# Context attention: the maximum over eight part maxima and the exponent's offset in one vector instruction, issued one copy later

## The chip, the core and the metric

The kernel runs on one core of one Trainium2 chip. The core has five engines that work side by side and meet through semaphores: PE (TensorE, matrix products), DVE (VectorE), ACT (ScalarE), POOL (GpSimd) and SP (SyncE, which here issues the DMAs). The metric is the device time of one execution in microseconds (us).

## What is computed

The reference is one perceiver layer: cross attention of 4 x 128 rows on a context of 8192 rows with 16 heads of 64, then a causal self attention, then a feed-forward layer with 4-bit weights. The change lies in the cross attention. Cut to that:

```
def _L0_xattn_ref(x, cond, Wq, bq, Wkv, bkv, Wp, bp):
    q = (x @ Wq + bq).reshape(1, B * N, H, hd)
    kv = (cond @ Wkv + bkv).reshape(1, -1, 2, H, hd)
    q = _fq_sym(q * scale, axis=-1)      # round to 127 levels per row and head
    k = _fq_sym(k, axis=-1)
    v = _fq_sym(v, axis=2)
    attn = softmax(einsum('bhqd,bhkd->bhqk', q, k), axis=-1)
    attn = _fq_unsigned(attn, axis=-1)   # scale so that the row's largest is 255, round
    out = einsum('bhqk,bhkd->bhqd', attn, v)
    return out @ Wp + bp
```

The kernel keeps q as integers and gives each score row a factor s (the row's query scale over K_SCALE). A probability in units of the row's largest/255 is exp(s * score + bias) with bias = ln 255 - s * (largest score of the row). LN_TOP is ln 255. The exponential is written as a 16-bit integer, which does the rounding.

## The kernel before

`attend_quantised` works in 64 **units** of one head (16) and 128 query rows (4 per head, T = 4). The score row of a unit has 8192 columns, cut in CH = 8 chunks of 1024. Two score rows (`at_sc0`, `at_sc1`) and two score banks in PSUM (`at_score0`, `at_score1`) are used in turn. For each unit:

- PE (`scores`) fills a bank with two 512-column products. It waits until the bank's last reader, two chunks earlier, is done.
- DVE (`copy`, L1508) copies the chunk from PSUM to `at_sc` and takes its maximum on the way into one column of `at_pmax`. In the trace this is a TENSOR_SCALAR_CACHE_REDUCE and a DVE_READ_ACCUMULATOR, which puts the maximum into SBUF. The chunks go in ORDER 2, 3, 6, 7, 4, 0, 1, 5; I call the copies p0 to p7 after their place in it. Each waits for its bank (`filled`) and for whoever still reads that part of `at_sc` for the unit two earlier: the exponentials, the DMA transpose, or PE's turns.
- DVE (`find_max`, L1513) reduces the eight part maxima to the negative maximum `at_nmax`, and (`make_bias`, L1520) turns it into `at_bias`. Both stand directly behind copy p7, and each waits for the instruction ahead of it.
- ACT (`exps`, L1598) takes the exponential of the two halves of the row in place, once `at_bias` is there. Behind each half stand two copies of the unit before, from PSUM to SBUF (`turned_out`, L1605).
- Half of each probability row is turned by a DMA transpose, the other half by PE in four groups (`turns`, k = 0 to 3, L1399), and PE multiplies them with the values (L1408, L1420). A turn k waits for `turned_out` of turn k - 2.
- Once per head, DVE also sums the row sums (`total_sum`, L1525), inverts them (L1529) and scales the output (L1535).

The order on each engine is written out by hand: `body(i, ...)` goes over the SLOTS = 8 units of one pair of heads and for each over c = 0 to 7. At slot c DVE copies chunk c + AHEAD (AHEAD = 2), so at c = 5 comes copy p7 of unit n + 1, and at c = 6 copy p0 of unit n + 2. The first and the last pair are written out, and the six pairs between them (48 units) run in a hardware loop, `Fori`, in which counts that grow with i are made in registers; DVE then has REGISTER_ALU and waiting instructions of its own between the copies.

POOL fetches each head's query columns and factors (`fetch`, `at_qs` from `exp_scale`, L1336), and quantises the values. `exp_scale` is made once, by `Queries.scales` (L639) in the key stage, more than 1100 us earlier.

Of the kernel before, what the change touches and what calls it, by code (L numbers as in the profile page):

```python
# [14 lines left out]
ALU = mybir.AluOpType  # L15
ACT = mybir.ActivationFunctionType
AX = mybir.AxisListType
F32 = mybir.dt.float32
# [4 lines left out]
P = 128  # L23
B, S, D = 4, 128, 1024
T = B * S // P
HEADS, HD = 16, 64
# [4 lines left out]
X_SCALE, W_SCALE, K_SCALE = 16.0, 256.0, 64.0  # L31
# [107 lines left out]
class Turner:  # L139
# [39 lines left out]
    def part(self, t, h):  # L179
        return slice(None), slice(4 * h, 4 * h + 4), slice(t * P, (t + 1) * P)  # L180
# [435 lines left out]
class Queries:  # L616
# [9 lines left out]
    def maximum(self, dve, t):  # L626

        self.nc.vector.tensor_reduce(self.amax[:, t, :], heads_of(self.q[:, t, :]), AX.X, ALU.max,
                                     apply_absolute_value=True).then_inc(self.scaled, 1)

    def scales(self, dve):

        nc = self.nc
        dve.wait_ge(self.scaled, T)
        nc.vector.tensor_scalar(self.scale[:], self.amax[:], HD ** -0.5 / LEVELS, 1e-8, ALU.mult, ALU.max)\
            .then_inc(self.scaled, 1)
        dve.wait_ge(self.scaled, T + 1)
        nc.vector.reciprocal(self.inv[:], self.scale[:]).then_inc(self.scaled, 1)
        nc.vector.tensor_scalar(self.exp_scale[:].rearrange("p h t -> p t h"), self.scale[:], 1.0 / K_SCALE, None,  # L639
                                ALU.mult).then_inc(self.scaled, 1)  # L640
        dve.wait_ge(self.scaled, T + 2)
        nc.vector.tensor_scalar(self.inv[:], self.inv[:], HD ** -0.5, None, ALU.mult).then_inc(self.scaled, 1)

    def divide(self, dve, t):

        dve.wait_ge(self.scaled, T + 4)
        rows = heads_of(self.q[:, t, :])
        self.nc.vector.tensor_tensor(rows, rows, per_head(self.inv[:, t, :]), ALU.mult).then_inc(self.scaled, 1)

    def round(self, dve):  # L650

        dve.wait_ge(self.scaled, 2 * T + 4)
        self.nc.vector.tensor_scalar(self.q[:], self.q[:], MAGIC, MAGIC, ALU.add, ALU.subtract).then_inc(self.scaled, 1)

    def scalar(self, act, c):

        act.wait_ge(self.scaled, 2 * T + 5)
        self.nc.scalar.activation(self.twice[:, :, :, c, :], self.q[:].rearrange("p t (h d) -> p t h d", d=HD),
                                  ACT.Copy).then_inc(self.step, 1)
# [549 lines left out]
def attend_quantised(chip, q_t, exp_scale, heads, v_scale, col, twice, o, ident32, ident16, x_d, x, stores, panels):  # L1209
# [7 lines left out]
    nc = chip.nc  # L1217
    SLOTS = 2 * T
    SC = 1024
    CH = NKV // SC  # L1220
# [3 lines left out]
    AHEAD = 2  # L1224
    LN_TOP = float(np.log(255.0))

# [7 lines left out]
    v_step, filled, copied = chip.sem("at_v_steps"), chip.sem("at_filled"), chip.sem("at_copied")  # L1234
    bias_ready, bias_step, exp_done = chip.sem("at_bias_ready"), chip.sem("at_bias_steps"), chip.sem("at_exp")
    dma_turned = [chip.sem(f"at_dma_turned{j}") for j in range(2)]
# [7 lines left out]
    COPIED0, EXP0, TURNED0, DMA0, OUT0, SUMMED0, DSUM0, INV0, TAKEN0, MOVED0 = 2, 4, 8, 16, 2, 4, 2, 4, 2, 2  # L1244
    with ExitStack() as ctx:
# [3 lines left out]
        q_pair = [chip.sb(ctx, f"at_q{j}", [P, T * P], F16) for j in range(2)]  # L1249
        qs_pair = [chip.sb(ctx, f"at_qs{j}", [P, T], F32) for j in range(2)]  # L1250
        vs_pair = [chip.sb(ctx, f"at_vs{j}", [P, HD], F32) for j in range(2)]
        vi_head = chip.sb(ctx, "at_vi", [P, HD], F32)
        o_pair = [chip.sb(ctx, f"at_o{j}", [P, T, HD], F32) for j in range(2)]
        part_max = [chip.sb(ctx, f"at_pmax{j}", [P, CH], F32) for j in range(2)]
        neg_max = [chip.sb(ctx, f"at_nmax{j}", [P, 1], F32) for j in range(2)]
        bias = [chip.sb(ctx, f"at_bias{j}", [P, 1], F32) for j in range(2)]
# [234 lines left out]
        def _(dve):  # L1491
# [18 lines left out]

            def find_max(h, n):
                dve.wait_ge(copied, COPIED0 + (h + 1) * CH)
                nc.vector.tensor_reduce(neg_max[n % 2][:], part_max[n % 2][:], AX.X, ALU.max, negate=True)\  # L1513
                    .then_inc(bias_step, 1)

            def make_bias(h, n):

                dve.wait_ge(bias_step, h + 1)
                j, t = (n % SLOTS) // T, n % T
                nc.vector.tensor_scalar(bias[n % 2][:], neg_max[n % 2][:], qs_pair[j][:, t:t + 1], LN_TOP,  # L1520
                                        ALU.mult, ALU.add).then_inc(bias_ready, 1)

# [15 lines left out]
            def body(i, first, last):  # L1538
                for n in range(SLOTS):
                    g = i * SLOTS + n  # L1540
                    for c in range(CH):
                        ahead, pos = (n + 1, c + AHEAD) if c + AHEAD < CH else (n + 2, c + AHEAD - CH)
# [3 lines left out]
                        j = (n // T + 1) % 2  # L1546
# [4 lines left out]
                        if done is not None and n % T == 1 and c == 4:  # L1551
                            output(done, j)
                        if c == 5 and not (last and ahead >= SLOTS):
                            find_max(i * SLOTS + ahead, ahead)
                            make_bias(i * SLOTS + ahead, ahead)

            for c in range(CH + AHEAD):
# [12 lines left out]
                if c == CH - 1:  # L1570
                    dve.wait_ge(q_ready, 2)
                    find_max(0, 0)
                    make_bias(0, 0)
# [669 lines left out]
def build(nc, a, out_d):  # L2243
# [11 lines left out]
    with chip.all, ExitStack() as whole:  # L2255
# [10 lines left out]
        with ExitStack() as cross:  # L2266
            q_t = chip.sb(cross, "q_t", [P, HEADS, T * P], F16)
            exp_scale = chip.sb(cross, "exp_scale", [P, HEADS, T], F32)
            v_scale = chip.sb(cross, "v_scale", [P, 2, D], F32)
# [150 lines left out]
```

## Time and profile before

| | us |
|---|---|
| median of 3 runs | 2665.52 (2664.87 to 2669.96) |
| span of the profiled execution | 2664.4 |
| PE busy in the span | 2483.9 (93%) |
| DVE busy in the span | 2035.2 (76%) |
| context attention, first to last `at_bias` | 1338.5 to 1967.6 |

The page gives the profiled execution by its span, from the first to the last instruction; the median lies 1.1 us above that. "Busy" counts the time of an engine's own instructions. Matrix products are pipelined and their ends modelled, so a busy PE need not be the limit. A bracket at the end of a timeline row is the idle time ahead of the instruction and whoever ended it.

### The profile page before, as it was taken

The numbers are of one execution on the slowest core, as the hardware profiler recorded it, in microseconds if no ns is written. First come the engines' busy times: TensorE is split into PE (matmuls) and PEld (weight loads), VectorE is DVE, ScalarE is ACT, GpSimd is POOL, SyncE is SP. The second block draws the span as 40 slices with busy tenths as digits, with TensorE's granted clock in tenths as the row PEclk, the third lists the DMA queues.
The fourth block names the chain that finished last, engine by engine and source line by source line (L and its number), as shares of the span: only waits on it lengthen the run. The fifth ranks groups of instructions, "written<-read, shape, count | busy, mean of one in ns | idle before, by whom it ended". The sixth has DMA issues, their size and how long they took to land. (4 is left out here: it accounts for less than half of the span.)

```text
span 2664.4 us, 42948 instructions
## 1 busy us (share of the span) xinstructions
PE 2483.9 (93%) x16296; PEld 1281.4 (48%) x16296; DVE 2035.2 (76%) x2932; ACT 1093.7 (41%) x1171; POOL 873.8 (33%) x432
## 2 busy tenths in 40 slices
PE   6999999999999999999978888888869999999998
PEld 3444444444444444444445555555544458444444
DVE  7898878778777877877699999999966344666664
ACT  4222222222222222222289999999982125211101
POOL 0233222322322232232166566566541651011100
PEclk9999999999999999999999999999999985999999
DMA  6234443443453344344479989989982331000000
GB/s 261 58 88 122 126 105 92 126 117 88 110 134 104 85 126 117 97 109 126 113 198 218 223 200 214 222 201 212 222 230 83 118 79 35 1 16 16 1 4 32
DMA packets 557347, 321.57 MB, mean 121 GB/s; under 512 B 401968, under 2 KB 533296, under 8 KB 552368
## 3 DMA queue, kind: packets, MB, share of 16 engines
q1 hardware_dynamic: 557232, 319.91, 47.0%
q8 instruction: 87, 1.43, 0.2%
q14 instruction: 28, 0.23, 0.0%
HBM read 149.95 MB, written 69.21 MB: 82 GB/s over the span
## 5 line engine op out<-in xcount | busy, mean ns | idle before, releaser
L1508 DVE TENSOR_SCALAR_CACHE_REDUCE at_sc<-at_score 128x1024 f32<-128x1024 f32 x512 | 597.1, 1220 | 12.5 <-PE at_score L1388 7.9
L1598 ACT ACTIVATE at_sc<-at_sc,at_bias,at_qs 128x4096 uint16<-128x4096 f32 x128 | 486.5, 3800 | 19.1 <-DVE at_bias L1520 18.4
L881 PE MATMUL kv_vacc<-wt_stage,kv_xthi 128*128 128x512 f16 x1024 | 388.1, 379 | 1.3 <-PEq L282 1.3
L881 PE MATMUL kv_vacc<-kv_wlo,kv_xthi 128*128 128x512 f16 x1024 | 388.1, 379 | 0.0
L881 PE MATMUL kv_vacc<-wt_stage,kv_xtlo 128*128 128x512 f16 x1024 | 388.1, 379 | 0.0
L889 PE MATMUL kv_kacc<-kv_wk,q_t 128*128 128x512 f16 x1536 | 347.2, 379 | 0.0
L960 ACT ACTIVATE q_t<-q_t 128x512 f16<-128x512 f32 x128 | 77.3, 628 | 488.9 <-POOL q_t L1163 327.8
L1161 POOL TENSOR_TENSOR q_t<-kv_rows 128x512 f32<-128x512 f32 x32 | 40.9, 1279 | 690.8 <-DMA kv_rows<-in_ctx 610.2
L889 PEld LDWEIGHTS kv_kacc<-kv_wk,q_t 128*128 128x128 f16 x1536 | 150.3, 98 | 181.2
L966 ACT ACTIVATE o<-wt_stage 128x1024 f16<-128x1024 f32 x64 | 67.7, 1058 | 407.0 <-DVE wt_stage L1052 407.0
L889 PE MATMUL kv_kacc<-kv_wk,kv_xthi 128*128 128x512 f16 x768 | 228.4, 379 | 0.7 <-DVE kv_xtlo L738 0.7
L1063 DVE SCALAR_TENSOR_TENSOR wt_stage<-kv_vacc,kv_bias 128x512 f32<-128x512 f32 x128 | 87.8, 686 | 175.9 <-PE kv_vacc L881 168.8
L1388 PE MATMUL at_score<-x,at_q 128*128 128x512 f16 x512 | 157.4, 390 | 61.2 <-DVE at_sc L1508 49.0
L1033 DVE SCALAR_TENSOR_TENSOR wt_stage<-kv_kacc,wt_stage 128x512 f32<-128x512 f32 x224 | 150.9, 686 | 80.6 <-PE kv_kacc L889 77.4
L1388 PE MATMUL at_score<-wt_stage,at_q 128*128 128x512 f16 x512 | 154.8, 384 | 53.6 <-DVE at_sc L1508 45.9
L1346 POOL TENSOR_TENSOR wt_stage<-wt_stage,at_vi 128x2048 f32<-128x2048 f32 x32 | 145.5, 4546 | 126.3 <-DMA wt_stage<-values 126.3
L1399 PEld LDWEIGHTS at_turn<-ident,at_sc 128*128 128x128 f16 x2048 | 136.4, 98 | 62.5 <-ACT at_sc L1598 2.9
L1028 DVE SCALAR_TENSOR_TENSOR q_t<-q_t 128x512 f16<-128x512 f32 x128 | 158.7, 1279 | 7.0 <-ACT q_t L960 7.0
L1174 POOL TENSOR_TENSOR wt_stage<-wt_stage,kv_bias 128x1024 f32<-128x1024 f32 x32 | 87.3, 2730 | 230.0 <-DVE wt_stage L1033 230.0
L1399 PE MATMUL at_turn<-ident,at_sc 128*128 128x128 f16 x2048 | 157.1, 220 | 3.2 <-ACT at_probt L1605 3.2
L881 PEld LDWEIGHTS kv_vacc<-wt_stage,kv_xthi 128*128 128x128 f16 x1024 | 100.2, 98 | 122.2 <-issue 1.7
L881 PEld LDWEIGHTS kv_vacc<-wt_stage,kv_xtlo 128*128 128x128 f16 x1024 | 100.2, 98 | 120.8
(246 smaller groups left out, 4242.6 us busy)
## 6 DMA issues: line engine op xcount, KB each, us to landing
kv_rows<-in_ctx SPq DMA_DIRECT2D x64, 512.0 KB, 7.0
values<-wt_stage SPq DMA_DIRECT2D x32, 1024.0 KB, 6.4
keys_turned<-o SPq DMA_DIRECT2D x32, 1024.0 KB, 5.1
wt_stage<-values SPq DMA_DIRECT2D x16, 2048.0 KB, 8.8
wt_stage<-keys_turned SPq DMA_DIRECT2D x32, 512.0 KB, 5.1
x<-keys_turned SPq DMA_DIRECT2D x31, 512.0 KB, 5.1
x<-in_x SPq DMA_DIRECT2D x2, 2048.0 KB, 8.6
kv_wk<-in_wq SPq DMA_DIRECT2D x2, 2048.0 KB, 12.7
```

Of the source, the lines that this page charges most:

```text
L881: last = nc.tensor.matmul(v_acc[2 * s + c][:], a[s][:, k, :], b[:, c, k, :], start=(k == 0 and q == 0), stop=(k == KD - 1 and q == 2))
L889: last = nc.tensor.matmul(k_acc[bank][:], a[:, k, :], b[:, k, :], start=(k == 0 and q == 0), stop=(k == KH - 1 and q == 2))
L960: nc.scalar.activation(s_hi[:, n], s_rows[:, n], ACT.Copy, scale=X_SCALE).then_inc(s_hi_ready, 1)
L1028: nc.vector.scalar_tensor_tensor(out=s_lo[:, n], in0=s_rows[:, n], scalar=X_SCALE, in1=s_hi[:, n], op0=ALU.mult, op1=ALU.subtract).then_in ...
L1033: nc.vector.scalar_tensor_tensor(out=out, in0=k_acc[bank][:], scalar=UNSCALE, in1=other, op0=ALU.mult, op1=ALU.add).then_inc(k_taken, 1)
L1063: nc.vector.scalar_tensor_tensor(out=val[:, h:h + HALF // HD, s, :], in0=v_acc[2 * s + c][:].rearrange("p (h d) -> p h d", d=HD), scalar=U ...
L1174: nc.gpsimd.tensor_tensor(key[:, 0, :], key[:, 0, :], bias[:, 0:D], ALU.add)\
L1346: nc.gpsimd.tensor_tensor(v_raw[:, tiles], v_raw[:, tiles], vi_head[:].unsqueeze(1).to_broadcast((P, KVT // 2, HD)), ALU.mult).then_inc(v_ ...
L1388: last = nc.tensor.matmul(score[pos % 2][:, b * HALF:(b + 1) * HALF], q_pair[j][:, t * P:(t + 1) * P], kt[j][:, cols], start=True, stop=True)
L1399: last = nc.tensor.transpose(turn[BANK[k]][:, b, :], prob[n % 2][1][:, at:at + P].bitcast(F16), ident16[:])
L1508: nc.vector.tensor_scalar(sc[n % 2][:, c * SC:(c + 1) * SC], score[pos % 2][:], 1.0, None, ALU.mult, ALU.max, accum_out=part_max[n % 2][:, ...
L1598: nc.scalar.activation(prob[n % 2][e], sc[n % 2][:, e * EC:(e + 1) * EC], ACT.Exp, bias=bias[n % 2][:], scale=qs_pair[j][:, t:t + 1], accu ...
```

## The change

The two small DVE instructions per unit become one `tensor_tensor_reduce`: it adds one column to the eight part maxima, multiplies by another, and takes the minimum. With c1 = -LN_TOP/s and c2 = -s, (m + c1) * c2 = LN_TOP - s * m, and its minimum over the parts is the bias. As a program it is two instructions, the main one and one that reads the accumulator into `at_bias`. It is issued at c = 6 instead of c = 5, behind copy p0 of the next unit but one; its wait for the copies stands with a semaphore increment of its own (`bias_begun`) ahead of it. `exp_scale` becomes three times as wide, with the two added columns from `Queries.scales`, and `at_qs` holds 12 elements instead of 4.

```
 class Queries:
+    def part(self, n):
+        return self.exp_scale[:, :, n * T:(n + 1) * T].rearrange("p h t -> p t h")
...
     def scales(self, dve):
...
-        nc.vector.tensor_scalar(self.exp_scale[:].rearrange("p h t -> p t h"), self.scale[:], 1.0 / K_SCALE, None,
-                                ALU.mult).then_inc(self.scaled, 1)
+        nc.vector.tensor_scalar(self.part(0), self.scale[:], 1.0 / K_SCALE, None, ALU.mult).then_inc(self.scaled, 1)
         dve.wait_ge(self.scaled, T + 2)
+        nc.vector.tensor_scalar(self.part(1), self.scale[:], -1.0 / K_SCALE, None, ALU.mult).then_inc(self.scaled, 1)
+        nc.vector.tensor_scalar(self.part(2), self.inv[:], -K_SCALE * LN_TOP, None, ALU.mult).then_inc(self.scaled, 1)
+        dve.wait_ge(self.scaled, T + 5)
...
-            def find_max(h, n):
-                dve.wait_ge(copied, COPIED0 + (h + 1) * CH)
-                nc.vector.tensor_reduce(neg_max[n % 2][:], part_max[n % 2][:], AX.X, ALU.max, negate=True)\
-                    .then_inc(bias_step, 1)
-
-            def make_bias(h, n):
-
-                dve.wait_ge(bias_step, h + 1)
+            def make_bias(h, n):
+
+                dve.wait_ge(copied, COPIED0 + (h + 1) * CH)
+                dve.sem_inc(bias_begun, 1)
                 j, t = (n % SLOTS) // T, n % T
-                nc.vector.tensor_scalar(bias[n % 2][:], neg_max[n % 2][:], qs_pair[j][:, t:t + 1], LN_TOP,
-                                        ALU.mult, ALU.add).then_inc(bias_ready, 1)
+                nc.vector.tensor_tensor_reduce(shifted[n % 2][:], part_max[n % 2][:],
+                                               qs_pair[j][:, 2 * T + t:2 * T + t + 1].to_broadcast((P, CH)),
+                                               qs_pair[j][:, T + t:T + t + 1], LARGEST, ALU.add, ALU.min,
+                                               bias[n % 2][:]).then_inc(bias_ready, 1)
...
-                        if c == 5 and not (last and ahead >= SLOTS):
-                            find_max(i * SLOTS + ahead, ahead)
-                            make_bias(i * SLOTS + ahead, ahead)
+                        if c == 6 and not (last and n + 1 >= SLOTS):
+                            make_bias(i * SLOTS + n + 1, n + 1)
```

How the instructions stand on DVE inside the loop, at the first unit of a head (the row sums of the head before are taken here). Before:

```order
L1508 TENSOR_SCALAR at_sc,at_pmax<-at_score 128x1024
L1524 ISA
L1525 TENSOR_REDUCE at_total<-at_psum 128x4
L1512 ISA
L1513 TENSOR_REDUCE at_nmax<-at_pmax 128x1
L1520 TENSOR_SCALAR at_bias<-at_nmax,at_qs 128x1
L1500 ISA
L1507 REGISTER_ALU
L1508 TENSOR_SCALAR at_sc,at_pmax<-at_score 128x1024
L1528 ISA
L1529 RECIPROCAL at_inv<-at_total 128x4
L1508 TENSOR_SCALAR at_sc,at_pmax<-at_score 128x1024
```

The same place after the change, with line numbers of the changed kernel (L1514 is the copy, L1522 the new instruction and its accumulator read):

```order
L1514 TENSOR_SCALAR at_sc,at_pmax<-at_score 128x1024
L1528 ISA
L1529 TENSOR_REDUCE at_total<-at_psum 128x4
L1506 ISA
L1513 ISA
L1514 TENSOR_SCALAR at_sc,at_pmax<-at_score 128x1024
L1532 ISA
L1533 RECIPROCAL at_inv<-at_total 128x4
L1519 REGISTER_ALU
L1522 ISA at_shifted,at_bias<-at_pmax,at_qs 128x8
L1522 ISA at_bias 128x1
L1514 TENSOR_SCALAR at_sc,at_pmax<-at_score 128x1024
```

Copy p0 has moved ahead of the offset, the offset stands behind the reciprocal too, and copy p1 follows it. In the key stage, DVE before:

```order
L635 TENSOR_SCALAR qq_scale<-qq_amax 128x64
L638 RECIPROCAL qq_inv<-qq_scale 128x64
L639 TENSOR_SCALAR exp_scale<-qq_scale 128x4x16
L642 TENSOR_SCALAR qq_inv<-qq_inv 128x64
L1063 SCALAR_TENSOR_TENSOR wt_stage<-kv_vacc,kv_bias 128x8x64
```

and after the change:

```order
L639 TENSOR_SCALAR qq_scale<-qq_amax 128x64
L642 RECIPROCAL qq_inv<-qq_scale 128x64
L643 TENSOR_SCALAR exp_scale<-qq_scale 128x4x16
L645 TENSOR_SCALAR exp_scale<-qq_scale 128x4x16
L646 TENSOR_SCALAR exp_scale<-qq_inv 128x4x16
L648 TENSOR_SCALAR qq_inv<-qq_inv 128x64
L1069 SCALAR_TENSOR_TENSOR wt_stage<-kv_vacc,kv_bias 128x8x64
```

Two instructions of 64 elements have come in ahead of a copy out of the value bank.

## Rows read from the trace of the kernel before

**Rows 1.** The profile's page: span, and busy us (share) of each engine.

```profile
span 2664.4 us, 42948 instructions
...
PE 2483.9 (93%) x16296; PEld 1281.4 (48%) x16296; DVE 2035.2 (76%) x2932; ACT 1093.7 (41%) x1171; POOL 873.8 (33%) x432
```

**Rows 2.** Window 1449 to 1938: busy us of PE, PEld, DVE, ACT, POOL; clock, DMA, GB/s.

```profile
1449.00:1938.00 489.00, 405.01 (x5516) 264.69 (x5514) 481.66 (x922) 473.37 (x396) 312.80 (x135) 1.00 0.92 211
```

**Rows 3.** Waits, 1340 to 1970 us: waiter <- releaser, us in total, times, longest.

```profile
DVE at_sc L1508 <- PE at_score L1388: 4.9, 3, 3.9
...
ACT at_sc L1598 <- DVE at_bias L1520: 18.4, 54, 0.8
```

**Rows 4.** Tile at_bias: ns min/median/max, first and last start.

```profile
L1520 DVE TENSOR_SCALAR at_bias<-at_nmax,at_qs x64: 212/214/216, 1338.5 to 1967.6; 128x1 f32<-128x1 f32 x64
```

**Rows 5.** Timeline of DVE in one head of the loop: start us, us, instruction.

```profile
1560.99 0.21 DVE L1520 TENSOR_SCALAR at_bias<-at_nmax,at_qs 128x1 f32<-128x1 f32 x1
1561.21 1.23 DVE L1508 TENSOR_SCALAR_CACHE_REDUCE at_sc<-at_score 128x1024 f32<-128x1024 f32 x1
...
1562.36 1.22 DVE L1508 TENSOR_SCALAR_CACHE_REDUCE at_sc<-at_score 128x1024 f32<-128x1024 f32 x1
...
1569.42 1.23 DVE L1508 TENSOR_SCALAR_CACHE_REDUCE at_sc<-at_score 128x1024 f32<-128x1024 f32 x1
...
1570.69 0.16 DVE L1513 TENSOR_REDUCE at_nmax<-at_pmax 128x1 f32<-128x8 f32 x1
1570.89 0.21 DVE L1520 TENSOR_SCALAR at_bias<-at_nmax,at_qs 128x1 f32<-128x1 f32 x1
1571.10 1.23 DVE L1508 TENSOR_SCALAR_CACHE_REDUCE at_sc<-at_score 128x1024 f32<-128x1024 f32 x1
...
1592.06 0.17 DVE L1529 RECIPROCAL at_inv<-at_total 128x4 f32<-128x4 f32 x1
1592.14 1.19 DVE L1508 TENSOR_SCALAR_CACHE_REDUCE at_sc<-at_score 128x1024 f32<-128x1024 f32 x1
```

**Rows 6.** Timeline of DVE at that head's end.

```profile
1598.99 0.42 DVE L1535 TENSOR_TENSOR at_o<-at_outp,at_inv 128x256 f32<-128x256 f32 x1
1599.32 1.22 DVE L1508 TENSOR_SCALAR_CACHE_REDUCE at_sc<-at_score 128x1024 f32<-128x1024 f32 x1
...
1600.78 0.21 DVE L1520 TENSOR_SCALAR at_bias<-at_nmax,at_qs 128x1 f32<-128x1 f32 x1
```

**Rows 7.** Timeline of ACT beside it: one unit.

```profile
1561.24 3.80 ACT L1598 ACTIVATE at_sc<-at_sc,at_bias,at_qs 128x4096 uint16<-128x4096 f32 x1 [0.48 <-DVE at_bias L1520]
...
1565.04 1.06 ACT L1605 ACTIVATE at_probt<-at_turn 128x512 int32<-128x512 int32 x2
1565.99 3.80 ACT L1598 ACTIVATE at_sc<-at_sc,at_bias,at_qs 128x4096 uint16<-128x4096 f32 x1
...
1569.78 1.07 ACT L1605 ACTIVATE at_probt<-at_turn 128x512 int32<-128x512 int32 x2
```

**Rows 8.** Timeline of PE in the same unit.

```profile
1567.52 0.61 PE L1399 MATMUL at_turn<-ident,at_sc 128*128 128x128 f16 x8
...
1568.66 0.61 PE L1399 MATMUL at_turn<-ident,at_sc 128*128 128x128 f16 x8
```

**Rows 9.** Timeline of DVE in the first pair of heads, outside the loop.

```profile
1372.98 0.21 DVE L1520 TENSOR_SCALAR at_bias<-at_nmax,at_qs 128x1 f32<-128x1 f32 x1
...
1381.20 1.23 DVE L1508 TENSOR_SCALAR_CACHE_REDUCE at_sc<-at_score 128x1024 f32<-128x1024 f32 x1
...
1382.80 1.21 DVE L1508 TENSOR_SCALAR_CACHE_REDUCE at_sc<-at_score 128x1024 f32<-128x1024 f32 x1
...
1412.03 0.21 DVE L1520 TENSOR_SCALAR at_bias<-at_nmax,at_qs 128x1 f32<-128x1 f32 x1
```

**Rows 10.** Timeline of DVE in the key stage, around the query scales.

```profile
200.95 0.55 DVE L638 RECIPROCAL qq_inv<-qq_scale 128x64 f32<-128x64 f32 x1
201.42 0.16 DVE L639 TENSOR_SCALAR exp_scale<-qq_scale 128x64 f32<-128x64 f32 x1
```

More of the change, by code:

```diff
@@ L24 @@
 B, S, D = 4, 128, 1024
+LN_TOP = float(np.log(255.0))
 T = B * S // P
@@ L638, in scales @@
         nc.vector.reciprocal(self.inv[:], self.scale[:]).then_inc(self.scaled, 1)
-        nc.vector.tensor_scalar(self.exp_scale[:].rearrange("p h t -> p t h"), self.scale[:], 1.0 / K_SCALE, None,
-                                ALU.mult).then_inc(self.scaled, 1)
+        nc.vector.tensor_scalar(self.part(0), self.scale[:], 1.0 / K_SCALE, None, ALU.mult).then_inc(self.scaled, 1)
         dve.wait_ge(self.scaled, T + 2)
+        nc.vector.tensor_scalar(self.part(1), self.scale[:], -1.0 / K_SCALE, None, ALU.mult).then_inc(self.scaled, 1)
+        nc.vector.tensor_scalar(self.part(2), self.inv[:], -K_SCALE * LN_TOP, None, ALU.mult).then_inc(self.scaled, 1)
+        dve.wait_ge(self.scaled, T + 5)
         nc.vector.tensor_scalar(self.inv[:], self.inv[:], HD ** -0.5, None, ALU.mult).then_inc(self.scaled, 1)
     def divide(self, dve, t):
-        dve.wait_ge(self.scaled, T + 4)
+        dve.wait_ge(self.scaled, T + 6)
         rows = heads_of(self.q[:, t, :])
@@ L650, in round @@
     def round(self, dve):
-        dve.wait_ge(self.scaled, 2 * T + 4)
+        dve.wait_ge(self.scaled, 2 * T + 6)
         self.nc.vector.tensor_scalar(self.q[:], self.q[:], MAGIC, MAGIC, ALU.add, ALU.subtract).then_inc(self.scaled, 1)
     def scalar(self, act, c):
-        act.wait_ge(self.scaled, 2 * T + 5)
+        act.wait_ge(self.scaled, 2 * T + 7)
         self.nc.scalar.activation(self.twice[:, :, :, c, :], self.q[:].rearrange("p t (h d) -> p t h d", d=HD),
@@ L1224, in attend_quantised @@
     AHEAD = 2
-    LN_TOP = float(np.log(255.0))
+    LARGEST = 3.0e38
     ORDER = (2, 3, 6, 7, 4, 0, 1, 5)
@@ L1234, in attend_quantised @@
     v_step, filled, copied = chip.sem("at_v_steps"), chip.sem("at_filled"), chip.sem("at_copied")
-    bias_ready, bias_step, exp_done = chip.sem("at_bias_ready"), chip.sem("at_bias_steps"), chip.sem("at_exp")
+    bias_ready, bias_begun, exp_done = chip.sem("at_bias_ready"), chip.sem("at_bias_begun"), chip.sem("at_exp")
     dma_turned = [chip.sem(f"at_dma_turned{j}") for j in range(2)]
@@ L1249, in attend_quantised @@
         q_pair = [chip.sb(ctx, f"at_q{j}", [P, T * P], F16) for j in range(2)]
-        qs_pair = [chip.sb(ctx, f"at_qs{j}", [P, T], F32) for j in range(2)]
+        qs_pair = [chip.sb(ctx, f"at_qs{j}", [P, 3 * T], F32) for j in range(2)]
         vs_pair = [chip.sb(ctx, f"at_vs{j}", [P, HD], F32) for j in range(2)]
@@ L1254, in attend_quantised @@
         part_max = [chip.sb(ctx, f"at_pmax{j}", [P, CH], F32) for j in range(2)]
-        neg_max = [chip.sb(ctx, f"at_nmax{j}", [P, 1], F32) for j in range(2)]
+        shifted = [chip.sb(ctx, f"at_shifted{j}", [P, CH], F32) for j in range(2)]
         bias = [chip.sb(ctx, f"at_bias{j}", [P, 1], F32) for j in range(2)]
@@ L1571, in _ @@
                     dve.wait_ge(q_ready, 2)
-                    find_max(0, 0)
                     make_bias(0, 0)
@@ L2267, in build @@
             q_t = chip.sb(cross, "q_t", [P, HEADS, T * P], F16)
-            exp_scale = chip.sb(cross, "exp_scale", [P, HEADS, T], F32)
+            exp_scale = chip.sb(cross, "exp_scale", [P, HEADS, 3 * T], F32)
             v_scale = chip.sb(cross, "v_scale", [P, 2, D], F32)
```

## The prediction

> **What bounds the kernel now.** I read the page first: the span is 2664.4 us and DVE is busy for 76% of it [rows 1], an average over stages. The tile of the offset then marks the stage that the change touches: 64 offsets, from 1338.5 to 1967.6 us [rows 4], so 629.1 us in 63 steps, 9.99 us per unit. In its middle DVE is busy for 481.66 of 489 us, ACT for 473.37 and PE for 405.01, at a granted clock of 1.00 (2.4 GHz) and with the DMA engines at 0.92 [rows 2]. The waits then say who sets the pace: ACT waits for `at_bias` 54 times, 18.4 us in all, while DVE waits for PE only 3 times, 4.9 us, of which one of 3.9 us is in the first units [rows 3]. So DVE runs without a real pause and ACT waits for its offset once per unit. The stage runs at DVE's pace, with ACT close behind.
>
> The timeline gives the sizes. In the loop one head takes from 1560.99 [rows 5] to 1600.78 [rows 6], 39.79 us, or 9.95 per unit. Copies follow each other after 1.15 us (1561.21 to 1562.36), though one lasts 1.23: the next starts 0.08 before the last has ended. From copy p7 (1569.42) to copy p0 (1571.10) it takes 1.68 [rows 5], so the maximum and the offset cost 1.68 - 1.15 = 0.53 us of DVE per unit. In that time lie 0.16 and 0.21 of work; the rest is the wait of each for the instruction ahead, and the waits of copy p0, which DVE gets to only behind the offset. In the pairs that are written out the same step takes 1.60, so it costs 0.45 there, and a head takes 1372.98 to 1412.03, 39.05 us [rows 9].
>
> ACT's own floor: first exponential to second 1561.24 to 1565.99, 4.75; from there to the next pair of copies 1569.78, 3.79; and that pair takes as long as the one at 1565.04, 0.95 to the next start [rows 7]. Together 9.49 us per unit, 37.96 per head. This is where a gain on DVE ends.
>
> **Part 1: the maximum and the offset leave the seam.** Per unit 0.53 us goes in the loop and 0.45 outside it. Copy p0 now follows p7 after 1.15: its own conditions (bank filled, exponential of two units earlier done) were met long before, since p0 of the trace waits for nobody. The new instruction's condition, the accumulator read of p7, is met in the first tenth of p0, so what DVE has to work through (a register instruction, the wait, the increment) lies beside the 1.15 us of p0.
>
> **Part 2: the new instruction behind p0.** No row shows a two-input reduction with an accumulator read. Nearest are the offset, one element with a scalar read per partition, 0.21, and the maximum over eight, 0.16 [rows 5]; I take 0.22. What it adds is less, since small instructions overlap as the copies do: the reciprocal of 0.17 moves the next copy from 1592.06 to 1592.14, by 0.08 [rows 5], and the output of 0.42 moves it from 1598.99 to 1599.32, by 0.33 [rows 6]. The accumulator read adds nothing behind a copy, since the next instruction starts with it. So c = 0.22 - 0.08 = 0.14 us. Bounds: from below nothing at all (the read and the work both covered), and 0.08 for an instruction as short as the maximum. From above 0.71: as long as the reciprocal of 64 elements, 0.55 [rows 10], with 0.08 lost overlap and 0.08 of read in full. I take 0.14, as the rows of its own size say.
>
> A rule speaks against that overlap. The rows above show starts 0.08 us ahead of the end of the instruction before. The Trainium skill, "VectorE: DVE Perf Modes", section "The DRAIN you can't avoid", says that the next operation does not start until the pipe has emptied; its section on two instructions with no wait between them lets one that isn't held start earlier. By the first the new pair would cost its full length each time, which is the rival with c = 0.30 below. The copies and the reciprocal of this trace go against it; that a reduction of this form behaves like them no row shows.
>
> **Part 3: row sums.** `total_sum` (once per head) was free, as it lay in the wait ahead of the maximum. Now copy p0 stands right behind it: 0.16 - 0.08, so 0.08 per head.
>
> **Sum.** In the loop DVE needs 39.79 - 4 x 0.53 + 4 x 0.14 + 0.08 = 38.31 us per head, 9.58 per unit, still above ACT's 37.96. Gain 1.48 per head, over 12 heads 17.8 us. Outside the loop DVE would need 39.05 - 1.80 + 0.56 + 0.08 = 37.89, under ACT's 37.96, so ACT sets it: gain 1.09, for three heads 3.3 us (of the fourth, its units lie ahead of the early stall of 3.9 us [rows 3], which POOL's first quantised values end, not DVE). Together 21.1 us.
>
> **What the moves do to others.** The offset of a unit now comes about 1.4 us later against the copies: 1.15 of p0 and 0.3 of its own. ACT's cycle shifts by that. Who waits for ACT? PE's turn k = 2 needs ACT's first copy out. It starts at 1567.52 [rows 8], 6.31 behind p0 at 1561.21; ACT's first copy would be done 1.4 + 0.04 + 3.80 + 0.53 = 5.8 behind p0. It has 0.5 us left, 0.65 with c added. Copies p2 and p3 need the second exponential, which ended at 1569.79, 1.3 us ahead of p0 [rows 7], and now ends about 0.1 behind it, two microseconds before p2. The DMA transpose is issued behind the first exponential and is read by PE and overwritten by DVE several microseconds later, so it has room. The DMA share goes from 0.92 to 0.92 x 9.95 / 9.58 = 0.96 [rows 2]; this is the term that I trust least. POOL works only part of each head. Behind the new instruction on DVE is queued copy p1, whose bank was filled during p0. The two extra instructions of the key stage are like the one of 0.16 us at 201.42 [rows 10] and happen once, at most 0.3 us; DVE has idle time in that stage. The fetch of 12 columns in place of 4 is POOL's and a head ahead. Both at nothing.
>
> The span becomes 2664.4 - 21.1 = 2643.3, and with the 1.1 us by which the median lies above the profiled span, **2644.4 us**.
>
> **Rivals.** I call 0.2%, 5.3 us, the smallest change that a measurement of this kernel can tell from none.
>
> (a) The new pair doesn't overlap, or DVE takes longer to get to it: c = 0.22 + 0.08 = 0.30. Loop 39.79 - 2.12 + 1.20 + 0.08 = 38.95, gain 0.84 x 12 = 10.1; outside 38.53, gain 0.52 x 3 = 1.6; time 2653.8. For it: the form is unseen, and in the loop the copy behind the offset starts only at its end (1570.89 + 0.21 = 1571.10). Against: outside the loop that delay is 0.08 smaller, so it comes from the waits of copy p0, which now stand elsewhere. Chance 0.2, from 2648 to 2660.
>
> (b) A circle through ACT takes over: offset, exponential and first copy out (0.04 + 4.33), PE's turns k = 2 and 3 up to copy p7 (1567.52 to 1569.42, 1.90), p7 and p0 (2.30), the new pair (0.30): 8.9 us for one unit. That is 0.7 below 9.58, so it should not bind; if DMA load and PE's queue stretch it by 0.9, the unit takes 9.8 and the loop gains 0.15 x 48 = 7, time 2656. Chance 0.08.
>
> (c) The change does not show in the total: the stage ends earlier, but what follows waits for weights or the DMA. 2665. The next weights are issued at fixed places of the same order and move along, so I see little for it. Chance 0.07, with mixed small effects.
>
> (d) Slower: the new instruction itself. Its place is behind p0 of each unit, its price c. It wins nothing from 4c + 0.08 = 2.12, c = 0.51. At the upper bound of 0.71 a head of the loop takes 40.59, 0.80 more, over 12 heads 9.6, and outside (40.17) 3.4 more: 2678.5. For it: the form is in no row, and the accumulator must be read on top. Against: the offset and the maximum, the nearest in size, last 0.21 and 0.16 [rows 5]. Chance 0.07.
>
> **Numbers.** My forecast has 0.58 and its own range is 2641 (c = 0.08: 38.07 per head, gain 20.6 + 3.3) to 2648. ACT's floor, 1.83 x 12 + 3.3 = 25.3, forbids anything much under 2640. For 8 in 10 I reach up to 2657, c = 0.35. Faster by over 0.2%: 0.58, nearly all of (a) and most of (b), 0.83. Within 0.2%: the rest of these and (c), 0.10. Slower: 0.07.
>
> **What would show it.** In the changed profile: p7 to p0 1.15 instead of 1.68; one small DVE row of about 0.22 us behind p0, p1 starting 1.29 behind p0; a loop head of 38.3 us; ACT busy near 99% in mid-stage, its waits for `at_bias` under 7 us; offsets from first to last in 608 us. I am wrong on the price if p0 to p1 takes 1.45 or more, wrong on the circle if DVE begins to wait ahead of p7 or PE for `at_probt`, and wrong on the bound if the head takes less but the total doesn't.

## The result and the profile after

The changed kernel takes 2736.91 us (median of 4 runs, 2736.24 to 2737.95), against 2666.34 of the kernel before (4 runs). The ratio is 1.026, with a 95% interval of 1.0245 to 1.0274: slower by 70 us, where I had forecast 21 us less. The profiled execution has a span of 2735.0.

The changed kernel's page answers to [rows 1]:

```profile
span 2735.0 us, 43013 instructions
...
PE 2514.2 (92%) x16296; PEld 1294.3 (47%) x16296; DVE 2098.9 (77%) x2934; ACT 1091.0 (40%) x1171; POOL 873.6 (32%) x432
```

DVE has 64 us more busy time for the same work: 2934 instructions instead of 2932, since the joined one runs as two, the main one and its accumulator read. POOL has what it had, 873.6 instead of 873.8. The window of mid-stage answers to [rows 2] (busy us of PE, PEld, DVE, ACT, POOL; clock, DMA share, GB/s):

```profile
1449.00:1938.00 489.00, 384.04 (x4948) 248.68 (x4946) 476.14 (x831) 424.22 (x353) 277.08 (x122) 0.96 0.84 191
```

DVE looks as full as before (476 of 489 us), yet 831 instructions stand in that window instead of 922, with as many per unit as before. Everybody else does less: ACT falls from 473 to 424 us, the DMA share from 0.92 to 0.84. A busy engine that finishes less is the first thing to see here.

The waits of the changed kernel from 1340 to 2045 us, beside [rows 3]:

```profile
ACT at_sc L1600 <- DVE at_bias L1522: 91.0, 33, 4.2
DVE at_sc L1514 <- PE at_score L1394: 13.5, 26, 0.9
```

ACT now waits 91.0 us for its offset, instead of 18.4 (33 times instead of 54, so each wait is far longer), and DVE 26 times for PE instead of 3. The tile of the new instruction takes the place of [rows 4] (duration ns min/median/max, first and last start):

```profile
L1522 DVE CUSTOM_DVE_ANT_0 at_shifted<-at_pmax,at_qs x64: 195/538/4524, 1339.4 to 2036.9; 128x8 f32<-128x8 f32 x64
```

The same instruction on the same eight elements lasts between 0.195 and 4.524 us, and next to no idle time stands ahead of it. The offsets take from 1339.4 to 2036.9, 697.5 us instead of 629.1; from the last offset to the end it is 698.1 us, against 696.8. So 68.4 of the 70.6 us of loss lie in this stage. The lengths come in a pattern of four units, one head. This is DVE in two heads of the loop (start us, us, instruction), which answers to [rows 5]:

```profile
1503.84 1.23 DVE L1514 TENSOR_SCALAR_CACHE_REDUCE at_sc<-at_score 128x1024 f32<-128x1024 f32 x1
...
1504.99 1.22 DVE L1514 TENSOR_SCALAR_CACHE_REDUCE at_sc<-at_score 128x1024 f32<-128x1024 f32 x1
...
1506.14 4.46 DVE L1522 CUSTOM_DVE_ANT_0 at_shifted<-at_pmax,at_qs 128x8 f32<-128x8 f32 x1
1510.53 0.08 DVE L1522 DVE_READ_ACCUMULATOR2_ANT at_bias<- 128x1 f32 x1
1510.53 1.21 DVE L1514 TENSOR_SCALAR_CACHE_REDUCE at_sc<-at_score 128x1024 f32<-128x1024 f32 x1
...
1520.94 1.51 DVE L1522 CUSTOM_DVE_ANT_0 at_shifted<-at_pmax,at_qs 128x8 f32<-128x8 f32 x1
...
1575.72 0.20 DVE L1522 CUSTOM_DVE_ANT_0 at_shifted<-at_pmax,at_qs 128x8 f32<-128x8 f32 x1
...
1584.19 1.22 DVE L1514 TENSOR_SCALAR_CACHE_REDUCE at_sc<-at_score 128x1024 f32<-128x1024 f32 x1
1585.33 0.22 DVE L1522 CUSTOM_DVE_ANT_0 at_shifted<-at_pmax,at_qs 128x8 f32<-128x8 f32 x1
...
1585.48 1.22 DVE L1514 TENSOR_SCALAR_CACHE_REDUCE at_sc<-at_score 128x1024 f32<-128x1024 f32 x1
```

And this is POOL over the same time:

```profile
1506.06 4.51 POOL L1352 TENSOR_TENSOR wt_stage<-wt_stage,at_vi 128x2048 f32<-128x2048 f32 x1 [9.66 <-DMA wt_stage<-values]
...
1517.88 4.54 POOL L1352 TENSOR_TENSOR wt_stage<-wt_stage,at_vi 128x2048 f32<-128x2048 f32 x1
...
1570.02 3.60 POOL L1358 TENSOR_TENSOR q_twice<-wt_stage,at_magic 128x2048 f16<-128x2048 f32 x1
1583.32 0.73 POOL L1364 TENSOR_TENSOR o<-at_o,at_vs 128x256 f32 x1 [9.70 <-DVE at_o L1539]
1584.00 0.61 POOL L1340 COPY at_q<-q_t 128x512 f16 x1
1584.55 0.19 POOL L1342 COPY at_qs<-exp_scale 128x12 f32 x1
1584.69 0.24 POOL L1346 COPY at_vs<-v_scale 128x64 f32 x1
1584.87 0.23 POOL L1347 COPY at_vi<-v_scale 128x64 f32 x1
```

Lay the ends over each other: the DVE instruction of 4.46 us ends at 1510.60 and POOL's at 1510.57; that of 1.51 us ends at 1522.45 and POOL's at 1522.42. At 1575.72 and 1585.33 POOL has nothing under way (it is through at 1573.62 and at 1585.10), and the same instruction takes 0.20 and 0.22. I took this count over all 64: 32 start while POOL is idle, and take 0.21 us on average (6.8 in all); 32 start while POOL is in one of its instructions on the values, every one of them is long (0.85 us at least), and every one ends 0.02 to 0.03 us after POOL's. There is no exception on either side. The 64 take 92.3 us, 78 more than at 0.22 each.

A stall costs more than its length. PE in the changed kernel, behind the stall of 4.46 us:

```profile
1511.80 1.03 PE L1394 MATMUL at_score<-x,at_q 128*128 128x512 f16 x2 [4.24 <-DVE at_sc L1514]
...
1515.33 0.60 PE L1394 MATMUL at_score<-x,at_q 128*128 128x512 f16 x2
```

The windows of these two rows, with the granted clock as the third number from the end:

```profile
1511.80:1515.00 3.20, 3.20 (x25) 2.09 (x26) 2.31 (x4) 3.20 (x4) 3.12 (x2) 0.51 0.02 5
1515.00:1520.00 5.00, 4.17 (x57) 2.50 (x55) 4.88 (x9) 5.00 (x6) 5.00 (x2) 1.00 0.93 174
```

PE stood idle for 4.24 us and then ran at a granted clock of 0.51, that is at 1.2 GHz, for some 3 us: the score pair takes 1.03 instead of 0.60. DVE, which never waited for PE there, then waits 0.90 us for it. So this head takes 14.80 + 10.95 + 9.61 + 9.50 = 44.86 us: the forecast's 38.31, plus 4.24 and 1.29 of the two long instructions, plus 1.0, about what DVE waits here for the slower PE.

### The profile page after: what moved, and what is told of

Its sections match the earlier page's. It is cut to its first block and busy times, and to the rows that moved or that the text cites. A ratio compares the mean times of both kernels' runs of the same rounds, so it can differ in the third digit from the quotient of the medians.

```text
span 2735.0 us, 43013 instructions
## 1 busy us (share of the span) xinstructions
PE 2514.2 (92%) x16296; PEld 1294.3 (47%) x16296; DVE 2098.9 (77%) x2934; ACT 1091.0 (40%) x1171; POOL 873.6 (32%) x432
## 5 line engine op out<-in xcount | busy, mean ns | idle before, releaser
L1514 DVE TENSOR_SCALAR_CACHE_REDUCE at_sc<-at_score 128x1024 f32<-128x1024 f32 x512 | 599.7, 1219 | 21.2 <-PE at_score L1394 16.5
L1394 PE MATMUL at_score<-x,at_q 128*128 128x512 f16 x512 | 165.2, 408 | 82.6 <-DVE at_sc L1514 68.3
L1405 PE MATMUL at_turn<-ident,at_sc 128*128 128x128 f16 x2048 | 162.9, 225 | 3.0 <-ACT at_probt L1607 3.0
```

The costliest lines, as they stand in the source:

```text
L1394: last = nc.tensor.matmul(score[pos % 2][:, b * HALF:(b + 1) * HALF], q_pair[j][:, t * P:(t + 1) * P], kt[j][:, cols], start=True, stop=True)
L1405: last = nc.tensor.transpose(turn[BANK[k]][:, b, :], prob[n % 2][1][:, at:at + P].bitcast(F16), ident16[:])
L1514: nc.vector.tensor_scalar(sc[n % 2][:, c * SC:(c + 1) * SC], score[pos % 2][:], 1.0, None, ALU.mult, ALU.max, accum_out=part_max[n % 2][:, ...
```

## The experiments

My theory from here on: the new instruction reads two tensors from SBUF, and such a DVE instruction cannot start its work while POOL is in an instruction of its own on SBUF; the profile shows this wait as duration. The rival at first: the reduction is a custom instruction and long by itself, or by how it is loaded. Each ratio below is against runs of the kernel before made beside it, with medians of 2666.6 to 2669.1 us.

**One SBUF input.** The offset at the same place with a plain instruction that has one tensor input and a scalar per partition. It leaves out the addition of ln 255.

```
-                nc.vector.tensor_tensor_reduce(shifted[n % 2][:], part_max[n % 2][:],
-                                               qs_pair[j][:, 2 * T + t:2 * T + t + 1].to_broadcast((P, CH)),
-                                               qs_pair[j][:, T + t:T + t + 1], LARGEST, ALU.add, ALU.min,
-                                               bias[n % 2][:]).then_inc(bias_ready, 1)
+                nc.vector.tensor_scalar(shifted[n % 2][:], part_max[n % 2][:], qs_pair[j][:, T + t:T + t + 1], None,
+                                        ALU.mult, ALU.min, accum_out=bias[n % 2][:]).then_inc(bias_ready, 1)
```

> The changed kernel with the offset made by a vector instruction that reads one tensor from SBUF (the stock tensor_scalar with an accumulator, (maximum of a part) * (-s), minimum over the parts) in place of the one that reads two; the place behind copy p0 is kept. It leaves out the addition of ln 255, nothing else. Theory A (in the changed kernel the new instruction waits for a POOL instruction that is under way, because it reads two tensors from SBUF; 27 of its 64 executions lasted over 1.3 us and most ended with a POOL instruction): no instruction of the offset lasts over 0.25 us, a loop head takes 38.3 us as the prediction had it, the time is 2645 us (2641 to 2650). Theory B (the accumulator form behind a copy's accumulator read is slow at this place, or the later place of the offset starves ACT and the stall only shows there): it still lasts 1.5 to 4.5 us in two units of four, 2725 to 2740 us.

Measured: 2653.76 us (4 runs), ratio 0.9952 (0.9935 to 0.9968). Its tile:

```profile
L1522 DVE TENSOR_SCALAR_CACHE_REDUCE at_shifted<-at_pmax,at_qs x64: 190/216/222, 1338.9 to 1953.7; 128x8 f32<-128x8 f32 x64
```

DVE in this kernel, while POOL multiplies the values (1527.25 to 1531.81):

```profile
1527.68 1.22 DVE L1514 TENSOR_SCALAR_CACHE_REDUCE at_sc<-at_score 128x1024 f32<-128x1024 f32 x1
...
1528.83 0.22 DVE L1522 TENSOR_SCALAR_CACHE_REDUCE at_shifted<-at_pmax,at_qs 128x8 f32<-128x8 f32 x1
...
1528.97 1.22 DVE L1514 TENSOR_SCALAR_CACHE_REDUCE at_sc<-at_score 128x1024 f32<-128x1024 f32 x1
```

All 64 last 0.19 to 0.22, though 47 of them start inside a POOL instruction. Second input gone, 83 us gone; the time is still 4 us above the 2650 that I had expected at most, of which more below. Its undisturbed head takes 9.66 + 9.60 + 9.50 + 9.50 = 38.26 us.

**The kernel before with one such instruction added.** The custom instruction went too in that run, so is it the cause? A plain `tensor_tensor` of 128 x 8 behind copy p0, with an output that nobody reads:

```
...
+                        if c == 6 and not (last and n + 1 >= SLOTS):
+                            j, t = ((n + 1) % SLOTS) // T, (n + 1) % T
+                            nc.vector.tensor_tensor(spare[n % 2][:], part_max[(n + 1) % 2][:],
+                                                    qs_pair[j][:, t:t + 1].to_broadcast((P, CH)), ALU.add)
```

> The kernel before, with one stock tensor_tensor of 128x8 added behind copy p0 of each unit, both inputs in SBUF (the part maxima and a broadcast column), its output unused; maximum and offset stay as they were. Theory A: it waits for POOL like the new instruction: in about half of the units it lasts 1 to 4.5 us, and the kernel comes to 2665 + 75 = 2740 us (2715 to 2760). Theory B (something peculiar to the new instruction): it lasts 0.16 us each time and adds 64 x 0.08 = 5 us, 2671 us.

Measured: 2728.14 us (2 runs), ratio 1.0229 (1.0209 to 1.025). Its tile:

```profile
L1556 DVE TENSOR_TENSOR at_spare<-at_pmax,at_qs x63: 133/165/3690, 1351.0 to 2025.8; 128x8 f32<-128x8 f32 x63
```

One instruction of 0.15 us of work per unit, used by nobody, costs the kernel before 62 us. The 32 that start with POOL idle take 4.8 us together, the 31 others 54.4, and each of these ends 0.02 to 0.03 us after POOL's instruction. The rival falls: two SBUF inputs are enough.

**POOL in pieces.** If DVE waits for the instruction under way, shorter ones must shorten the wait. The changed kernel, with each of POOL's passes over the values cut in 4:

```
+            QT = KVT // 8
...
-                    nc.gpsimd.tensor_tensor(v_raw[:, tiles], v_raw[:, tiles], rounder, ALU.add).then_inc(v_step, 1)
+                    for q in parts_of(half):
+                        last = nc.gpsimd.tensor_tensor(v_raw[:, q], v_raw[:, q], rounder, ALU.add)
+                    last.then_inc(v_step, 1)
```

> The changed kernel, with each of POOL's passes over half a head's values cut in four instructions of a quarter of the size (128x512 instead of 128x2048, about 1.1 and 0.9 us instead of 4.5 and 3.6). Theory A: no offset instruction lasts longer than one piece and itself, 1.4 us; with about 0.6 us of wait in every second unit the sum over 64 falls from 92 us to some 30, and the time to 2660 us (2648 to 2672). Theory B: POOL's size doesn't matter, the long ones stay at 1.5 to 4.5 us, 2725 to 2745 us.

Measured: 2675.59 us (7 runs), ratio 1.003 (1.0018 to 1.0041); and with 16 pieces:

> As e2_pieces4, with sixteen pieces per pass (128x128 each). The computation is the reference's. Theory A: the wait is at most one piece, 0.3 us, so the 64 offset instructions last at most 24 us in all instead of 34, and the time is 2653.8 + 24 - 13.5 = 2664 us or less (2656 to 2668), unless the small pieces make POOL late. If POOL becomes late, PE waits for q_twice and the time is above 2680.

Measured: 2773.08 us (4 runs), ratio 1.0397 (1.038 to 1.0415). The tile with 4 pieces, and then with 16:

```profile
L1530 DVE CUSTOM_DVE_ANT_0 at_shifted<-at_pmax,at_qs x64: 215/570/1285, 1339.4 to 1975.1; 128x8 f32<-128x8 f32 x64
```

```profile
L1530 DVE CUSTOM_DVE_ANT_0 at_shifted<-at_pmax,at_qs x64: 214/444/3395, 1338.9 to 2076.3; 128x8 f32<-128x8 f32 x64
```

With 16 pieces, mid-stage (columns as in the window above):

```profile
1449.00:1900.00 451.00, 350.39 (x4440) 227.17 (x4437) 401.46 (x743) 381.76 (x317) 376.40 (x998) 0.92 0.81 186
```

Four pieces take 61 us back: the longest of the 64 falls from 4.5 to 1.3, their sum from 92.3 to 34.1, as expected. The time was expected to reach 2672 at most and is 3.6 us above that; the stage's first seven units take 81.1 us there, against 74.4 in the one-input kernel. Sixteen pieces lose it all and more: POOL is busy for 376 of 451 us, and PE waits 38.7 us in that window for POOL's quantised values. The longest is 3.4 us there, so it is not always one piece that DVE waits for. The 64 of that trace fall in two kinds: 49 last 0.57 us or less, and the 15 others, 0.74 to 3.4, all end with the last piece of a multiplication pass. Why DVE gets in between two pieces in one case and not in the other stays open.

**What was the place worth, and what the joining?** The kernel before with its own two instructions moved behind copy p0, and the one-input form put back at the old place behind p7:

```
-                        if c == 5 and not (last and ahead >= SLOTS):
-                            find_max(i * SLOTS + ahead, ahead)
-                            make_bias(i * SLOTS + ahead, ahead)
+                        if c == 6 and not (last and n + 1 >= SLOTS):
+                            find_max(i * SLOTS + n + 1, n + 1)
+                            make_bias(i * SLOTS + n + 1, n + 1)
```

> The kernel before, with its own two instructions (maximum, then offset, one SBUF tensor each) moved behind copy p0, not joined. Theory A: no waits for POOL. The 0.12 us that the maximum waited for the accumulator read goes, and most of its 0.16 overlaps, so a loop unit needs about 9.95 - 0.53 + 0.35 = 9.77 us: 2665 - 0.18 x 48 - 2 = 2655 us (2649 to 2661). Theory B in the form that the later place of the offset is what costs: slower than 2665, with ACT and PE waiting for each other.

Measured: 2661.65 us (10 runs), ratio 0.9982 (0.9973 to 0.9992), just above the expected range. The one-input form at the old place differs from the first experiment in one line:

```
-                        if c == 6 and not (last and n + 1 >= SLOTS):
+                        if c == 5 and not (last and n + 1 >= SLOTS):
```

> As e1_one_input (one SBUF tensor, accumulator form, the addition of ln 255 left out), but at the old place, directly behind copy p7. It tells the joining from the moving. No wait for POOL in either theory. If joining alone saves the second instruction and its wait: the accumulator read of p7 (0.12) and 0.22 stay exposed, 0.35 to 0.40 us a unit instead of 0.53 in the loop, so 2665 - 0.15 x 48 - 1 = 2657 us (2653 to 2661). If the gain of e1_one_input comes from the place alone: 2665 us.

Measured: 2669.61 us (10 runs), ratio 1.0009 (0.9999 to 1.0018). DVE in this kernel, from copy p7 to copy p0:

```profile
1568.74 1.23 DVE L1514 TENSOR_SCALAR_CACHE_REDUCE at_sc<-at_score 128x1024 f32<-128x1024 f32 x1
...
1570.16 0.22 DVE L1522 TENSOR_SCALAR_CACHE_REDUCE at_shifted<-at_pmax,at_qs 128x8 f32<-128x8 f32 x1 [0.18 <-DVE at_sc L1514]
...
1570.42 1.22 DVE L1514 TENSOR_SCALAR_CACHE_REDUCE at_sc<-at_score 128x1024 f32<-128x1024 f32 x1
```

From p7 to p0 it takes 1570.42 - 1568.74 = 1.68 us, exactly the kernel before's, although the two instructions are joined there. I had expected the joining to bring a gain by itself; at the old place it brings none. Behind p0 the two forms differ: a loop head takes 38.96 us with two instructions (9.81 + 9.80 + 9.68 + 9.67) and 38.26 with one.

**The 9 us that the one-input form lacks.** It should have come to 2644.4 by the prediction's sum. Eight of the loop's 48 units take 10.1 to 10.4 us instead of 9.50 to 9.66; that is some 5 of the 9 us. PE there, in the one-input kernel:

```profile
1531.40 0.60 PE L1394 MATMUL at_score<-wt_stage,at_q 128*128 128x512 f16 x2
1533.05 0.64 PE L1426 MATMUL at_outp<-q_twice,at_probt_dma 128*128 128x64 f16 x16 [1.05 <-DMA at_probt_dma<-at_sc]
```

PE waits for a row that the DMA turns. I thought of the DMA load as such (share 0.95), and cut the stage's key loads to a quarter, which leaves most keys unloaded (and ln 255 out, as before):

```
-            sp.dma_start(self.kt[j][:, q * n:(q + 1) * n],
+            sp.dma_start(self.kt[j][:, q * n:q * n + n // width],
...
-                        heads.keys(sp, 2 * i + j + 2, j, QUARTERS[0])
+                        heads.keys(sp, 2 * i + j + 2, j, QUARTERS[0], 4)
```

> As e1_one_input, with the key loads inside the stage cut to a quarter of their columns (the rest of the keys stays as it was). It tells where the 8 us are that e1_one_input lacks to the predicted 2644.4: PE waited there 21 times for at_probt_dma, 23 us on its weight loads, and about one unit in eight was 0.6 to 0.95 us longer. If the DMA engines, busy for 0.95 of the time, make the transposes late: these waits go, a unit takes 9.57 throughout, 2646 us (2643 to 2649). If not: 2653 us.

Measured: 2653.87 us (4 runs), ratio 0.9949 (0.9932 to 0.9965). The window of mid-stage:

```profile
1449.00:1900.00 451.00, 389.11 (x5229) 250.82 (x5230) 442.99 (x876) 446.50 (x374) 299.63 (x127) 1.00 0.81 177
```

PE's wait for the turned rows in it:

```profile
PE at_outp L1426 <- DMA at_probt_dma<-at_sc: 8.5, 10, 1.2
```

The share is 0.81 and nothing has changed: PE waits 8.5 us, against 9.3 with all keys loaded. The load of the keys is not it. What stood next to the late rows in SP's order was the 2 MB load of the values, issued just ahead of them. I split that in two halves at neighbouring units, in the one-input form and in the moved form:

```
+                    if n == (3 if first else 2):
+                        heads.values(sp, 2 * i + 1, (1,))
...
+                    if n == T + 2 and not last:
+                        heads.values(sp, 2 * i + 2, (1,))
...
-                pool.wait_ge(v_loaded, 16 * head + 16)
+                pool.wait_ge(v_loaded, 32 * head + 32)
```

> This is the kernel with the one-input offset behind copy p0 (it leaves out the addition of ln 255 to the exponent), in which the 2 MB load of a head's quantisation values, once per head, is issued as two loads of 1 MB at two neighbouring units. The kernel it starts from takes 2653.8 us, with a loop head of 38.3 us except that about once per head one unit takes 10.0 to 10.4 us, because PE waits for a transposed row; 7 to 8 us in all. Theory (the late transposes are those queued right behind the values load): each transpose finds half of the load ahead of it, the wait of up to 1.3 us shrinks under what PE has in hand, long units (over 9.9 us) become rare: 2647 to 2650. Rival (the load's size has no part in it, it is the two transposes and the place in the order): the long units stay, 2653 to 2655.

> The same split of the values load, but with the maximum and the offset as the two instructions of the kernel before, both behind copy p0 (complete computation). Without the split it takes 2661.7 us, its units 9.67 to 9.81 us with one of 10.05 to 10.50 per head. Theory (late transposes behind the values load): about 4 us of it go, 2656 to 2658. Rival (no part): 2661 to 2663.

Measured: 2682.01 us (5 runs), ratio 1.0052 (1.0038 to 1.0067), and 2683.97 us (5 runs), ratio 1.0064 (1.005 to 1.0077): both far from either theory. PE's waits of the first, 1449 to 1900 us:

```profile
PE at_outp L1421 <- POOL q_twice L1365: 17.6, 7, 3.5
...
PE at_outp L1433 <- DMA at_probt_dma<-at_sc: 0.5, 3, 0.2
```

The waits for turned rows are gone (0.5 us instead of 9.3), so the theory held for them; but POOL waited for both halves before it took the first, began a unit later, and PE waited 17.6 us for it (one unit in eight takes 11.2 to 14.1 us, and two of the stage's first seven 19.6 and 16.4). I had not followed the moved load to its reader. The mend is a wait of POOL for each half by itself:

```
-                pool.wait_ge(v_loaded, 32 * head + 32)
                 for half in range(2):
+                    pool.wait_ge(v_loaded[half], 16 * head + 16)
```

> The kernel with the one-input offset (it leaves out the addition of ln 255) and the values load split in two halves at neighbouring units, in which POOL waits for each half by itself and so starts on the first one a unit earlier than it did with the split load. With the split alone (2682.0) all units but one in eight took 9.50 to 9.66 us, and that one 11.2 to 14.1, because PE waited for POOL's second half (7 waits, 17.6 us). Theory (the size of the load ahead of the transposes was what made the long units of 10.0 to 10.4; the split's own price was POOL's late start): both are gone, every unit 9.50 to 9.66, time 2652.0 to 2646, I take 2646. Rival (POOL's second half still comes late, or the early units of the stage, 12.6 to 19.6 us with the split, hold the loss): above 2655.

> The same with the maximum and the offset as two instructions behind copy p0 (complete computation). Without the split 2661.7 us, units of 9.67 to 9.81 and one of 10.05 to 10.50 per head. Theory: the long units go, about 4 to 6 us less, 2656 to 2658, the fastest complete kernel of this study. Rival: no gain or a loss by POOL, 2661 or more.

Measured: 2648.63 us (5 runs), ratio 0.9931 (0.9917 to 0.9945) for the one-input form, and 2659.41 us (6 runs), ratio 0.9968 (0.9956 to 0.998) for the moved one. In the first no unit of the loop is longer than 9.66 any more (38.26 per head, twelve times); the first seven units of the stage take 76.6 us, against 74.4 with the load in one piece and 73.5 in the kernel before, and so keep 3 us. Whether the smaller piece or the later place of the second half ended the waits, these runs do not separate. Its window:

```profile
1449.00:1900.00 451.00, 393.97 (x5275) 253.13 (x5274) 447.01 (x886) 450.87 (x379) 300.95 (x127) 1.00 0.97 220
```

ACT is busy for 450.87 of 451 us, so hardly anything is left between the 38.26 of a head and the prediction's floor of 37.96, and that at a DMA share of 0.97, higher than in any other kernel here. The moved form with halves, 2659.41 us, has the lowest time of those that compute everything; it was expected at 2656 to 2658, and its interval (0.9956 to 0.998) overlaps that of the moved form without halves (0.9973 to 0.9992). A form with the part maxima elsewhere than in SBUF, which would keep the joined instruction out of POOL's way, was not tried.

## Why the prediction was wrong

- **Part 1** (0.53 us leave the seam) was right: from p7 to p0 it takes 1.15 us in the changed kernel (1503.84 to 1504.99), and units without a long instruction take 9.61 and 9.50.
- **Part 2 is the step that failed.** I took c = 0.14, with 0 to 0.71 as bounds. It is 0.15 with POOL idle (1585.33 to 1585.48) and 4.39 in the long one shown (1506.14 to 1510.53); on average 92.3/64 - 0.08 = 1.36 us, nearly twice the upper bound. The nearest rows, offset, maximum and reciprocal [rows 5, 10], are all instructions with one tensor input from SBUF; in the trace of before 61 of the 64 offsets start inside an instruction of POOL and none lasts over 0.22. I looked for the nearest in size and operation, where the number of SBUF operands decided.
- **What the moves do to others** has the line that hid it: "POOL works only part of each head". It does, about 300 of 451 us, and I took that as a reason for POOL not to matter, without asking what the new instruction shares with it.
- **Rival (d)** had the side, slower, and the break-even, c = 0.51, but priced an instruction that is long by itself, at 2678.5. It had a chance of 0.07. With c = 1.36 its own formula gives 39.79 - 2.12 + 5.44 + 0.08 = 43.19 per head, 3.40 more, 41 us over twelve heads and some 11 over the other three, near 2718. A head of the loop in fact takes 44.26 on average: 1.07 more, 13 us, which for one head the rows above show as PE's slow clock behind a stall and DVE's wait for it. The last 6 us lie near the first pair: the first seven units take 79.0 us instead of 73.5, where I had counted nothing.
- **Part 3 and the sum** were right for what they cover: 38.31 forecast, 38.26 measured in the undisturbed heads of the one-input kernels. Outside the loop, the first head of the last pair takes 37.93 in the one-input kernel with halves, where I had ACT's 37.96.
- **The DMA term**, the one I trusted least, was worth something, but not through the share that I had worked out: cutting the key loads did nothing, and splitting the one transfer ahead of the turned rows brought 5 of the 9 us that the one-input kernel lacked (2653.76 to 2648.63).

The evidence stood in the trace of before, in the key stage, where DVE and POOL also meet. This is DVE's product of two SBUF tensors there, twice:

```profile
609.27 2.79 DVE L1056 TENSOR_TENSOR o<-wt_stage,o 128x1024 f16<-128x1024 f32 x1
...
619.75 1.22 DVE L1056 TENSOR_TENSOR o<-wt_stage,o 128x1024 f16<-128x1024 f32 x1
```

POOL beside the first of them:

```profile
608.23 2.75 POOL L1174 TENSOR_TENSOR wt_stage<-wt_stage,kv_bias 128x1024 f32<-128x1024 f32 x1 [7.33 <-DVE wt_stage L1033]
```

The tile of DVE's product:

```profile
L1056 DVE TENSOR_TENSOR o<-wt_stage,o x64: 1217/1274/2792, 108.4 to 1315.8; 128x1024 f16<-128x1024 f32 x64
```

The first begins inside POOL's instruction, which ends at 610.98, and ends at 612.06, 1.1 us later, about one normal length; the second begins with POOL idle and takes 1.22. The instruction's tile shows it in one row: a largest duration of more than twice the smallest, for one shape. It is no accident of one moment: 31 of the 64 last 2.78 or 2.79, and each starts inside that instruction of POOL. It takes two inputs in SBUF: the DVE instruction of L1033, with one of its two inputs in PSUM, starts 109 times inside an instruction of POOL and never lasts over 0.69. From this the forecast could have followed: POOL is at work for about two thirds of the stage (312.80 of 489 us, [rows 2]), so two or three of a head's four new instructions meet it (in the changed kernel it was 32 of 64, two per head), and each then waits until POOL's is over.

The same trace shows two more things. POOL waits for DVE as well:

```profile
2110.52 6.42 POOL L1644 TENSOR_TENSOR space<-space,rope_swapped 128x1024 f32<-128x1024 f32 x1
```

```profile
2108.84 5.88 DVE L267 SCALAR_TENSOR_TENSOR wt_ring<-wt_stage,wt_ring 128x4096 f16<-128x4096 f32 x1 [3.02 <-ACT wt_ring L262]
```

Six of the eight of POOL's L1644 take 2.34 to 2.35 us. The other two begin inside a DVE instruction with two SBUF inputs, last 6.41 and 6.42, and end 2.2 us after it. And one SBUF input is not always safe:

```profile
L1889 DVE TENSOR_SCALAR space<-space x68: 412/420/1397, 2264.4 to 2610.0; 128x512 int32<-128x512 int32 x68
```

Eleven of these 68 start inside an instruction of POOL, and all eleven last 1.39 to 1.40 us instead of 0.41 to 0.42.

The rule is written down. The Trainium skill, "SBUF — State Buffer", section "Who interferes with whom", states that a DVE instruction with two SBUF inputs contends with a GpSimd instruction that reads SBUF, and that one with at most one SBUF input, outside the two-port modes, does not contend. Its section "SBUF: two separate sides" adds that whoever starts first gets the shared port pair for the whole instruction. The 64 of the changed kernel (32 of 32 long with POOL at work, 0 of 32 without) and the 64 of the one-input kernel (0 of 47) agree with the first two, the ends of the long instructions on both engines with the third. Whether L1889 runs in one of the two-port modes no view here tells; it takes 0.42 us for 128 x 512 elements, where the two-input form of L1028 takes 0.68.

## What to carry to other kernels

Before pricing an instruction that does not stand in a trace, count its SBUF tensor inputs and look for the nearest instruction with the same count; if that one's longest duration is far above its smallest, find who is at work during the long ones. Joining two cheap one-input instructions into one with two inputs can cost far more than it saves on an engine that works beside POOL. And when a load is moved or split, follow it to its reader's wait first.

## What the runs showed of the hardware that I had not expected

- The wait of a two-input DVE instruction for POOL stands inside its duration, as busy time: 0.22 us of work shown as up to 4.52. The views of waits and of idle time do not name it; only minimum and maximum, and the coincidence of the ends, do. It works in both directions (POOL's 6.42 us instead of 2.35), and an int32 instruction with one SBUF input can meet it too (1.39 instead of 0.42).
- A pause of 4.24 us on PE is followed by some 3 us at a granted clock of 0.51, with score pairs of 1.03 us instead of 0.60.
- At the old place, the joined instruction costs what the two did, 1.68 us from copy to copy; 0.18 of it stands in the trace as its wait for the copy ahead, and its work there is 0.22.
- With a 2 MB load issued right ahead of two turning DMAs, PE waits up to 1.3 us for the turned rows, at a DMA share of 0.81 as well as 0.95; with two loads of 1 MB, one ahead of each, its waits for them come to 0.4 us in the same window instead of 9.3.
